# One core, a masked four-head attention layer: the first batch's loads, writes and reads in another order

## What is computed

```python
# per batch b of 8: N = 1500 nodes, F = 64 features, H = 4 heads of 16; adj is a 0/1 matrix of 1500 x 1500
feats   = einsum('nf,hfo->hno', x, kernel)
f_self  = einsum('nf,hfd->hnd', x, attention_kernel)
f_other = einsum('nf,hfd->hdn', x, attention_kernel_2)
scores  = einsum('hnd,hdm->hnm', f_self, f_other)
masked  = adj * scores
masked  = where(masked >= 0, masked, 0.2 * masked) / 4 + where(adj == 0, -1e9, 0)
attn    = softmax(masked, axis=-1) * (adj != 0)
y       = relu(einsum('hnm,hmo->hno', attn, feats) + bias)     # heads side by side: 1500 x 64
out     = layernorm(x + y)
```

## Time and profile before

| | us |
|---|---|
| Median of 3 runs (lowest, highest) | 906.92 (906.81, 907.31) |
| The profiled execution | 912.7 |
| Span of its trace | 910.8 |
| First instruction of the first group on PE | 50.18 |
| PE busy in the span | 835.0 (92%) |

### The profile page before, as it was taken

The page is one execution under the profiler, slowest core; times in us unless marked ns, Lnnn a source line. Parts: engine busy times, 40 slices in busy tenths (PEclk is TensorE's granted clock), DMA queues, the critical chain, the costliest instruction groups (busy, mean ns, idle before and its releaser), DMA issues.

```text
span 910.8 us, 14879 instructions
## 1 busy us (share of the span) xinstructions
PE 835.0 (92%) x4668; PEld 259.5 (28%) x4668; DVE 774.7 (85%) x1422; ACT 780.0 (86%) x1553; POOL 657.8 (72%) x643
## 2 busy tenths in 40 slices
PE   4079998999989999999999999899999999899993
PEld 3022332233323332233323332232322333222220
DVE  3176998889978899989999899799999899899993
ACT  2078997899978999999989999799999999799992
POOL 5065886758877698858888599676888589766654
PEclk9589999899999999999999999999999999999996
DMA  9794689908798098935898098962999278990301
GB/s 239 136 233 123 120 187 221 239 8 218 122 257 196 0 249 160 264 119 119 192 254 227 1 233 130 265 163 52 235 203 245 57 199 137 243 196 18 48 1 36
DMA packets 198402, 144.57 MB, mean 159 GB/s; under 512 B 177104, under 2 KB 177104, under 8 KB 198320
## 3 DMA queue, kind: packets, MB, share of 16 engines
q1 hardware_dynamic: 195152, 139.91, 66.2%
q10 hardware_dynamic: 3168, 3.67, 2.4%
HBM read 94.08 MB, written 12.51 MB: 117 GB/s over the span
## 4 chain that ended last, share of the span: by engine, by line
PE 77%; DMA 7%; DVE 5%; ACT 3%; SPq 3%; issue 2%; POOL 2%; ACTq 1%; POOLq 0%; DVEq 0%
PE z L536 45%; PE numer L567 26%; DMA maskT<-mask 3%; SPq L239 3%; DVE z L850 2%; PE misc L471 2%; ACT probs L766 2%; DMA parts_dram<-part 2%; PE misc L511 1%; PE misc L477 1%; DMA w_val<-in_L_gnn_kernel 1%; SPq L231 1%; DVE probs L850 1%; PE misc L464 1%; ACT squares L707 1%
## 5 line engine op out<-in xcount | busy, mean ns | idle before, releaser
L850 DVE SCALAR_TENSOR_TENSOR z<-z,maskT 128x512 f32<-128x512 f32 (+1 forms) x864 | 557.4, 678 | 62.4 <-PE z L536 54.9
L536 PE MATMUL z<-self_st,other_st 96*128 96x512 bf16 (+3 forms) x2016 | 521.1, 381 | 39.7 <-issue 24.1
L386 POOL TENSOR_TENSOR probs<-probs,lows 128x512 f32<-128x512 f32 (+1 forms) x288 | 360.5, 1252 | 220.3 <-ACT probs L760 211.0
L766 ACT ACTIVATE probs<-z 128x512 f32<-128x512 f32 (+1 forms) x864 | 462.6, 602 | 52.0 <-PE z L536 43.2
L536 PEld LDWEIGHTS z<-self_st,other_st 96*128 96x128 bf16 (+1 forms) x2016 | 169.8, 98 | 494.4 <-ACT probs L766 223.1
L567 PE MATMUL numer<-probs,vals 128*32 128x512 f32 (+1 forms) x2304 | 304.8, 601 | 3.0 <-POOL probs L386 2.8
L850 DVE SCALAR_TENSOR_TENSOR probs<-z,maskT 128x512 f32<-128x512 f32 (+1 forms) x288 | 191.0, 663 | 41.3 <-PE z L536 25.5
L759 ACT ACTIVATE lows<-z 128x512 f32<-128x512 f32 (+1 forms) x288 | 177.3, 616 | 43.7 <-DVE probs L850 43.0
L760 ACT ACTIVATE probs<-probs 128x512 f32<-128x512 f32 (+1 forms) x288 | 187.1, 650 | 0.0
L344 POOL TENSOR_SCALAR mask<-edges 128x1500 int16<-128x1500 f32 x96 | 138.6, 1444 | 10.4 <-DMA edges<-in_adj 2.7
L567 PEld LDWEIGHTS numer<-probs,vals 128*32 128x32 f32 x2304 | 45.6, 108 | 98.9 <-ACT probs L766 75.4
(11 more groups left out here) (70 smaller groups left out, 270.2 us busy)
## 6 DMA issues: line engine op xcount, KB each, us to landing
edges<-in_adj SPq DMA_DIRECT2D x88, 750.0 KB, 5.8
parts_dram<-part SPq DMA_DIRECT2D x21, 384.0 KB, 7.0
self_st<-parts_dram SPq DMA_DIRECT2D x42, 192.0 KB, 5.6
other_st<-parts_dram SPq DMA_DIRECT2D x42, 192.0 KB, 5.8
edges<-in_adj SPq DMA_DIRECT2D x8, 468.8 KB
x_sb<-in_x SPq DMA_DIRECT2D x8, 352.0 KB
out<-cent SPq DMA_DIRECT2D x8, 352.0 KB
maskT<-mask SPq DMA_TRANSPOSE x96, 6.0
```

The lines of the kernel that those rows point to most:

```text
L386: pool.tensor_tensor(p, p, lows[:, g % 2, 0:WIDTH[st]], ALU.mult).then_inc(pooled, 1)
L536: return nc.tensor.matmul(z[:, v % BUFS * STEP + i, 0:WIDTH[st]], other_st[par][rows, h, c * P:(c + 1) * P], self_st[par][rows, h, st * W: ...
L766: nc.scalar.activation(slot, bank, ACT.Exp, scale=LOW).then_inc(expd, 1)
L850: return nc.vector.scalar_tensor_tensor(out, z[:, v % BUFS, 0:WIDTH[st]], FLOOR, maskT[(par + st) % 2][:, c, 0:WIDTH[st]], ALU.max, ALU.mult)
```

## The change

`first_read` is new and replaces `first_stack`. SP issues the edges of strip 0 only when all six weight loads have landed. ACT issues the three writes without any read between them. The reads are cut by strips of 512 columns into 64 KB each (36 instead of 12): ACT issues the 18 of `other_st`, SP, behind its transposes, the 18 of `self_st`, in both cases strip by strip, and waits for each part's write once. PE waits for strip 0 before the first group, for strip 1 before the 5th and for strip 2 before the 9th. SP waits for strip 1 before it issues the edges of strip 1. ACT runs one exponential of a single element before the bias load.

```diff
+        def first_read(queue, k, st, dst, part_of, row):
+            cols = slice(st * W, (st + 1) * W)
+            if st == 0:
+                queue.wait_ge(first_out[k], 16)
+            for g in range(len(part_of)):
+                if part_of[g] == k:
+                    queue.dma_start(dst[g * D:(g + 1) * D, :, cols],
+                                    parts_dram[k, row:row + HF, cols].rearrange("(h d) n -> d h n", h=H)
+                                    ).then_inc(first_stacks[st], 16)
...
@@ sync
             load_x(0, 0)
+            sp.wait_ge(weights_in, 96)
             for j in range(SJ):
                 load_edges(0, 0, j)
             for j in range(SJ):
                 sp.wait_ge(mask_made, j + 1)
                 turn(0, 0, j)
-            sp.wait_ge(stacks_in, 16 * STACK_DMAS)
+            for st in range(NS):
+                for k in range(3):
+                    first_read(sp, k, st, self_st[0], SELF_PART, 0)
+            sp.wait_ge(first_stacks[1], 16 * STACK_DMAS)
             for j in range(SJ):
                 load_edges(0, 1, j)
...
@@ tensor
+                    if first and not large and n in (SJ, 2 * SJ):
+                        pe.wait_ge(first_stacks[n // SJ], 16 * STACK_DMAS)
...
-                pe.wait_ge(stacks_in, at(b, 16 * STACK_DMAS, 16 * STACK_DMAS))
+                if first:
+                    pe.wait_ge(first_stacks[0], 16 * STACK_DMAS)
+                else:
+                    pe.wait_ge(stacks_in, 16 * STACK_DMAS * b)
...
@@ scalar
+            act.wait_ge(table, 1)
+            nc.scalar.activation(warm[:, :], warm[:, :], ACT.Exp)
             act.dma_start(bias_rep[:, :], ...
...
             act.wait_ge(first_part[0], NS)
-            act.dma_start(parts_dram[0, :, :], parts[0][:, :]).then_inc(parts_out, 16)
+            act.dma_start(parts_dram[0, :, :], parts[0][:, :]).then_inc(first_out[0], 16)
...
-            first_stack(0)
             for k in (1, 2):
                 act.wait_ge(first_part[k], NS)
-                act.dma_start(parts_dram[k, :, :], parts[k][:, :]).then_inc(parts_out, 16)
-                first_stack(k)
+                act.dma_start(parts_dram[k, :, :], parts[k][:, :]).then_inc(first_out[k], 16)
+            for st in range(NS):
+                for k in range(3):
+                    first_read(act, k, st, other_st[0], OTHER_PART, HF)
+            act.sem_inc(parts_out, 48)
...
@@ vector
+            dve.memset(warm[:, :], 0.0).then_inc(table, 1)
```

More of the change, by code:

```diff
@@ L114, in gat_layer @@
         bias_rep = sb("bias_rep", [P, HF], F32)
+        warm = sb("warm", [1, 1], F32)
         ident = sb("ident", [P, P], F32)
@@ L162, in gat_layer @@
         x_in = sem("x_in")
+        table = sem("table")
+        first_out = [sem(f"first_out{k}") for k in range(3)]
+        first_stacks = [sem(f"first_stacks{k}") for k in range(NS)]
         edges_in = [sem(f"edges_in{j}") for j in range(SJ)]
@@ L597, in groups @@
             def groups(b, par, first, last, large):
+                if large and first:
+                    for st in range(1, NS):
+                        pe.wait_ge(first_stacks[st], 16 * STACK_DMAS)
                 if large:
@@ L714, in numer_out @@
                 nc.scalar.copy(o_sb[:, :], numer[:, 0:W]).then_inc(numer_free, 1)
[L716 to L726, removed]
             for r in range(XT_ROUNDS):
```

## The result

The changed kernel takes 902.94 us (median of 8 runs, 899.83 to 907.65) against 908.91 for the kernel before on the same chip (8 runs, 906.81 to 912.21): a ratio of 0.9923, 95% interval 0.9895 to 0.9951. It is faster by 0.8%: the ratio stands for 7 us, the medians lie 6.0 apart. That is less than half of the 15.6 that were forecast, and outside the forecast range. The profiled execution took 903.3 us, its span 901.3.

What follows compares the result with a forecast made beforehand. PE, 92% busy, bounds the kernel; its idle time is concentrated in the start, behind weights, projection and three DRAM round trips. First group 18.7 us earlier, 3.1 given back: -15.6, from 906.92 to 891.3 us, 8-in-10 range 885 to 898.

Steps and rivals of the forecast that it cites:

- Weights, projection, ACT: Start of the kernel: weights landed at 8.4, ACT ready at 8.6, projection at about 8.7, 7.1 us earlier.
- Part 2 and write 2: After projection, at the old distances: part 2 ready at 17.8, write 2 out at about 17.9, ACT's reads from 18.3.
- SP through the transposes at 22.4, bounds 21.6 to 22.9: SP's queue: edges wait for weights, first tile lands at 12.6, transposes take 8.84 us, then SP's reads can be issued.
- SP's first byte moves 0.9 us behind its issue: SP's first read of strip 0: its bytes start moving at 23.3.
- I take 155 GB/s: Rate of the strip reads on two queues: 5.1 us a strip, strip 0 seen landed at 29.9.
- The ends, 101 and 291: Bounds on the read rate in GB/s: the slowest slice gave 101, issuing 64 KB every 0.45 us on two queues allows 291.
- (A): How much earlier than 50.18 PE's first group starts: 18.7 us, at 31.5.
- (B), the give-back: POOL's first mask of strip 1: edges land at 39.2, 7.7 us behind the start, so 3.1 us are given back.
- 6 us behind what the weights alone would allow: SP ready for its reads about 6 us later than the weights alone would allow, the price of holding edges back.
- Slow reads: Rival: reads at 101 GB/s, 7.8 us a strip, start 34.2, total 896.8; 0.22 with late weights or strips not coming apart.
- Strips do come apart: Rival denied here: later reads overtake, start waits for all 2.36 MB, 37.5, total 894.2; within a shared 0.22.
- The price by the read: Rival: each read costs 1.33 us whatever its size, 0.33 us a packet, start 42.5, total 913; chance 0.04.

Runs made afterwards that it cites:

- experiment 3: Changed kernel with ACT's reads waiting until all four transposes have landed: 895.0 us (one execution), first group at 38.04.
- experiment 5: Four tries, three without SP's wait for the weights: ACT's reads later 895.9 us, other strip order 900.1, other band order 892.5; changed kernel, all reads after transposes, 902.6.
- experiment 2: Changed kernel with strip 1's edges issued on SP right behind strip 0's reads, without a wait: 904.02 us against 914.39 for the kernel before, ratio 0.9888.
- the first experiment: Changed kernel with its reads not cut into strips, 12 of 192 KB on both queues, all waited for: 927.3 us (one execution).

## Why the prediction was wrong

**Weights, projection, ACT: right.** Landed by 7.47 (8.4 forecast), projection 8.39 (8.7), write 0 at 13.55 (14.2), the exponential 0.20 us.

**Part 2 and write 2: wrong, without effect.** Ready at 20.5, not 17.8. The prediction carried the "old distances" over. DVE's splits, to be set beside 1.10 and 1.89 us for the same three instructions each without the hold, and POOL beside them:

```profile
14.28 3.23 DVE L957 CAST part<-rest 128x512 bf16<-128x512 f32 x3
17.43 3.11 DVE L961 TENSOR_TENSOR part<-rest,part 128x512 bf16<-128x512 f32 x3
...
15.78 1.45 POOL L364 TENSOR_SCALAR mask<-edges 128x1500 int16<-128x1500 f32 x1 [0.46 <-DMA edges<-in_adj]
18.24 1.76 POOL L364 TENSOR_SCALAR mask<-edges 128x1500 int16<-128x1500 f32 x1 [1.01 <-DMA edges<-in_adj]
```

The hold has moved POOL's masks over DVE's splits, and both are stretched; without the hold the masks are over by 16.3. That they hinder each other is read from this coincidence; no run took the masks away. ACT's reads could start late at no loss (experiment 3), so it cost nothing.

**"SP through the transposes at 22.4, bounds 21.6 to 22.9": the first failed step, 3.9 us.** They took 12.76 us, not 8.84. The bounds came from one set of rows, in which nothing but edge loads ran beside the transposes, and I moved the block into the time of the writes. In eight kernels without the hold (the one before among them) it took 8.7 to 8.9 us; in those with it 11.0 to 14.6, and 20.7 beside large reads. Reads are not needed for it (12.54 without any). Nor are the masks, the last of which was made by 20.0. The three writes are the nearest company: their landing went from 2.3 to 3.0 us (without the hold) to 3.8 to 5.5, and with one write beside them (the hold alone) the transposes took 11.0 us, with three at least 12.1. That it is the writes was not tried apart.

**"SP's first byte moves 0.9 us behind its issue": the second, 2.9 us.** It moved at 30.1, 3.8 us behind. The prediction asked when the transposes would be issued, and of their landing only whether DVE's mask was there; it put at nothing that SP's reads queue behind them. The last transpose landed at 32.2, 8.5 us behind its issue where 4.0 to 6.2 was read the earlier trace rows, and SP's first read at 33.3. Without the hold the transposes have landed 1.5 to 2.7 us before SP's first read is issued.

**"I take 155 GB/s": the third, 2.3 us.** From SP's first byte to the landing of strip 0 it took 8.9 us, where 5.1 + 1.5 = 6.6 was forecast. The row behind it (148) was a single queue's. Two queues of reads were never in the trace of before; with the hold they moved 112 to 147, without it 167 to 194. Why the same reads move at one rate or the other is open (experiment 5). The ends, 101 and 291, held the value, but the late transposes stood on top of it.

Together 3.9 + 2.9 + 2.3 = 9.1 us: the start at 40.70 instead of 31.5. Three quarters of it are the transposes. (A) was 9.5, not 18.7.

**(B), the give-back: right in mechanism and, by luck, in size.** The edges went out 4.65 us behind the start and were found at 8.9, against 3.5 and 7.7 forecast. The distance from the first group to the ruler grew by 60.35 - 57.25 = 3.1 us, the forecast's figure, and experiment 2 took just that away. -9.5 + 3.1 = -6.4 is the ruler's shift, and the repeated runs say -7.

**The price of the hold: the error behind them.** The prediction did call it "6 us behind what the weights alone would allow", but took the rest of the change's gain as resting on the early weights. It doesn't. With the hold off, the same kernel gains 15.3 us by the ruler and 1.65% in repeated runs, which is the forecast's size, by luck; in the changed kernel SP's reads waited for the transposes, and the early projection bought nothing. Write 2 at 24.4 and SP free at 19.3 fit each other far better than 20.6 and 26.3 do. No rival named this. "Slow reads" (101 GB/s, 896.8) came nearest, and the measured median lies 6.1 us above it.

**The other rivals.** Strips do come apart: strip 0 landed at 39.0, strip 1 at 45.3. The price by the read, 1.33 us whatever its size, is refuted (over both queues a 64 KB read every 0.57 us at 115 GB/s, and every 0.34 us at 194). Nor does each read pay 2 us after the one before: SP's landed 1.1 us apart.

## What to carry to other kernels

Before a load is held back to speed up another, ask what the held load feeds and into whose time all of that moves; here 8 us of idle waiting for weights was the best place for edges, masks and transposes, since nothing else wanted the queues. A duration read from a trace holds for the company it had: when a block of DMAs is moved, its bounds have to come from rows with the new company, and what queues behind such a block waits for its landing, not for its issue. Cutting a transfer so that work can start on its first piece was worth more in this kernel than anything done to its bandwidth, and what feeds the second piece then has to be issued between the pieces, late enough not to stand in front of what is needed next.

## What the runs showed of the hardware

- SP's issue of four DMA transposes of 128 x 1,536 16-bit values takes 8.7 to 8.9 us with edge loads alone beside them, 11.0 to 14.6 with writes, and 20.7 us with reads of 192 KB on the other queue.
- A read issued on a queue whose transposes have not landed moves nothing until they are nearly through: 3.8 us behind its issue in the changed kernel, 11.7 us in the first experiment, 1.4 us where they had landed.
- Reads of DRAM into 16 partitions: 116 to 175 GB/s on one queue, 112 to 194 on two, with the engines taken to the same share (1.12 to 1.18) at both ends of the second range. Into 32 partitions, 211 to 213 on two.
- The same three DVE instructions took 1.10 and 3.23 us, 1.89 and 3.11, the longer ones where POOL's masks ran beside them.
